# Order of the first stores and loads in an attention and mixture-of-experts kernel, and later batches in its last quad

## The reference

```
Q, K, V = xn @ W.T + bias           # 16 heads of 16 features
S[i, j] = K_i . Q_j / 4  + (-(i - j)), and -inf where j > i
s       = softmax(S) @ V, heads joined, @ o_w.T + o_b
probs   = softmax(xn @ gate_w); the best 2 of 8 experts, scores renormalised
f       = sum over the two experts of alpha_e * score * (gelu(xn @ fc1_e + b1_e) @ fc2_e + b2_e)
out     = x + s * silu(f)
```

## Time and profile before

| | |
|---|---|
| median of 3 runs | 718.47 us (714.88 to 721.5) |
| the profiled execution | 721.25 us |
| its span in the trace | 719.4 us |
| TensorE busy in the span | 681.2 us (95%) |
| VectorE, ScalarE, POOL busy | 535.6, 484.8, 236.3 us |
| bytes moved by DMA | 124.46 MB, 173 GB/s in the mean |

### The profile page before, as it was taken

How to read it: one execution, slowest core, us unless ns; L and a number is a source line. 1 busy time by engine, 2 the same in 40 slices (tenths; PEclk the granted TensorE clock), 3 DMA queues, 4 the chain that set the end, 5 groups by cost and what they waited for, 6 DMA issues and landing times.

```text
span 719.4 us, 17538 instructions
## 1 busy us (share of the span) xinstructions
PE 681.2 (95%) x6042; PEld 460.7 (64%) x6042; DVE 535.6 (74%) x1146; ACT 484.8 (67%) x994; POOL 236.3 (33%) x336
## 2 busy tenths in 40 slices
PE   6994999999999999999999999999789999999985
PEld 4873766555565556556555655654359998999764
DVE  6563887999989999998998999896224554444298
ACT  4551443677877877788787778878776666666374
POOL 5331211234023424323342432300034757566300
PEclk9996999999999999999999999999999999999998
DMA  6899976243765686477568657610369786955396
GB/s 213 267 259 312 330 225 200 79 65 87 106 138 138 136 173 148 124 170 156 137 140 174 140 130 164 166 28 19 89 132 259 255 195 219 233 182 174 121 391 248
DMA packets 74903, 124.46 MB, mean 173 GB/s; under 512 B 14184, under 2 KB 44392, under 8 KB 74696
## 3 DMA queue, kind: packets, MB, share of 16 engines
q1 hardware_dynamic: 65200, 95.17, 51.9%
q0 software_dynamic: 9616, 28.17, 12.7%
HBM read 72.56 MB, written 49.72 MB: 170 GB/s over the span
## 4 chain that ended last, share of the span: by engine, by line
PE 81%; DVE 9%; DMA 4%; issue 3%; ACT 2%; POOL 0%; SPq 0%; POOLq 0%; DVEq 0%; ACTq 0%
PE ps L1588 20%; PE ps L1519 14%; PE ps L1572 13%; PE ps L1676 8%; PE ps L1698 8%; PE ps L1508 7%; PE ps L1468 5%; DVE mxa L1111 3%; PE ps L1478 3%; PE ps L1659 2%; DVE x_room L1425 1%; DVE arena L1420 1%; DMA q_parts<-arena 1%; DVE arena L1410 1%; DMA arena<-xs_dram 1%
## 5 line engine op out<-in xcount | busy, mean ns | idle before, releaser
L1111 DVE TENSOR_REDUCE mxa<-ps 128x1 f32<-128x512 f32 (+3 forms) x608 | 358.3, 655 | 45.4 <-PE ps L1508 30.9
L972 ACT ACTIVATE arena<-ps 128x512 f32<-128x512 f32 x576 | 303.7, 603 | 83.1 <-PE ps L1572 42.9
L1519 PE MATMUL ps<-aug 57*128 57x512 f32 (+3 forms) x768 | 218.6, 403 | 11.7 <-issue 9.1
L1572 PE MATMUL ps<-aug 59*128 59x512 f32 (+3 forms) x768 | 215.3, 398 | 0.5 <-ACT arena L972 0.5
L1588 PE MATMUL ps<-arena,v_q 128*32 128x512 f32 (+3 forms) x1536 | 154.4, 497 | 6.7 <-ACT arena L972 6.3
L1572 PEld LDWEIGHTS ps<-aug 59*128 59x128 f32 x768 | 109.4, 185 | 75.9 <-ACT arena L972 70.3
L1519 PEld LDWEIGHTS ps<-aug 57*128 57x128 f32 x768 | 110.0, 188 | 47.4 <-DVE mxa L1111 24.3
L867 POOL DMA_INDIRECT xs_dram<-arena,slot x64 | 62.6, 978 | 75.6 <-ACT arena L972 71.7
L894 POOL DMA_INDIRECT y_dram<-arena,y_row_of x71 | 69.4, 977 | 52.4 <-DVE y_row_of L1349 45.2
L1508 PE MATMUL ps<-key_mask,key_rows 64*128 64x64 bf16 (+2 forms) x704 | 79.7, 209 | 0.0
L1676 PE MATMUL ps<-arena 128*128 128x128 f32 x568 | 75.2, 275 | 0.0
(11 more groups left out here) (149 smaller groups left out, 642.1 us busy)
## 6 DMA issues: line engine op xcount, KB each, us to landing
aug<-k_parts SPq DMA_DIRECT2D x96, 128.0 KB
aug<-q_parts SPq DMA_DIRECT2D x96, 128.0 KB
arena<-xs_dram SPq DMA_DIRECT2D x71, 128.5 KB, 2.6
k_parts<-arena SPq DMA_DIRECT2D x16, 512.0 KB, 4.7
q_parts<-arena SPq DMA_DIRECT2D x16, 512.0 KB, 5.6
arena<-y_dram SPq DMA_DIRECT2D x16, 512.0 KB, 6.7
xn_dram<-arena SPq DMA_DIRECT2D x8, 512.0 KB, 6.3
a_dram<-arena SPq DMA_DIRECT2D x128, 32.0 KB
```

The source lines that it names most:

```text
L972: nc.scalar.activation(prob_slot(q, i), score_bank(q, i), ACT.Exp).then_inc(exp_done, 1)
L1111: nc.vector.tensor_reduce(dst, src, AX.X, ALU.max).then_inc(piece_used, 1)
L1519: ins = nc.tensor.matmul(banks[:, at_ * width:(at_ + 1) * width], k_aug[n][rows, hp, ib * P:(ib + 1) * P], q_aug[n][rows, hp, lo:lo + widt ...
L1572: ins = nc.tensor.matmul(out_[:, col0:col0 + hi - lo], q_aug[n][rows, h // SIDES_OF_ARRAY, jb * P:(jb + 1) * P], k_aug[n][rows, h // SIDES ...
```

## The change

It has five parts. `SIDES` becomes K m0, Q m0, K m1, Q m1. The stores of sequence 0's m0 parts count on semaphores of their own (`first_parts_out`), and all twelve loads of quad 0 are issued in one go at the end of chunk 1, when the two m0 stores of each half have landed. The late constants move from behind chunk 0 to behind chunk 5; the masks stay and get a semaphore of their own. The waits follow these moves: `parts_stored(b)` replaces `16 * 4 * (b + 1)`, the first item waits for `masks_in`, and the wait for `consts_in` stands before the windows on TensorE and VectorE. Six batches and a seventh of the last window are sent one to three units later.

```diff
-LAST_BATCH_AFTER = (6, 11, 15, 19, 23, 27, 31, NU - 1)
+LAST_BATCH_AFTER = (7, 13, 18, 22, 26, 30, 33, NU - 1)
...
+def parts_stored(b):
+
+    return 16 * (4 * (b + 1) - 2 * (b > 0))
...
-        SIDES = [(side, m) for side in range(2) for m in range(KT)]
+        SIDES = [(side, m) for m in range(KT) for side in range(2)]
...
-                                 parts[c][n]).then_inc(parts_out[c], 16)
-                    if b == PLAIN and c == 0 and n < 2:
-                        if n == 0:
-                            for half in range(CHUNKS):
-                                sp.wait_ge(parts_out[half], 16 * 4 * (PLAIN + 1))
-                        for g in range(NLOAD // 2 * n, NLOAD // 2 * (n + 1)):
-                            load_rows(0, 0, g)
-                    if n == (1 if b == PLAIN and c == 0 else 0) and more > 0:
+                                 parts[c][n]).then_inc(first_parts_out[c] if b == 0 and m == 0 else parts_out[c], 16)
+                    if n == 0 and more > 0:
                         store_normalised(i + 1, b + c, 1 - c)
                     if b in (PLAIN + 1, PLAIN + 2) and c == 0:
+                        if b == PLAIN + 2 and n == 0:
+                            for half in range(CHUNKS):
+                                sp.wait_ge(parts_out[half], parts_stored(1))
                         for g in range(NLOAD // 4 * n, NLOAD // 4 * (n + 1)):
                             load_rows(b - PLAIN, b - PLAIN, g)
+                if b == 0 and c == 1:
+                    for half in range(CHUNKS):
+                        sp.wait_ge(first_parts_out[half], 16 * 2)
+                    for g in range(NLOAD):
+                        load_rows(0, 0, g)
...
                     if b == 0 and c == 0:
+                        load_masks()
+                    if b == PLAIN + 1 and c == 1:
                         for name in LATE_CONSTS:
                             sp.dma_start(*loads[name]).then_inc(consts_in, 16)
-                        load_masks()
...
-                act.wait_ge(parts_out[c], 64 * b + 64)
+                act.wait_ge(parts_out[c], parts_stored(b))
+                if b == 1:
+                    act.wait_ge(first_parts_out[c], 16 * 2)
...
+                if i == 0 and m == 0 and side == 1:
+                    pe.wait_ge(weights_high, 3)
...
-                            pe.wait_ge(consts_in, 16 * NCONST)
+                            pe.wait_ge(masks_in, 16 * NMASK)
```

More of the change, by code:

```diff
@@ L179 @@
 LATE_CONSTS = ("num", "before", "alpha", "wo", "ob", "vb")
-NCONST = SIDES_OF_ARRAY * len(CONSTS) + len(LATE_CONSTS)
+NMASK = SIDES_OF_ARRAY * len(CONSTS)
+NCONST = len(LATE_CONSTS)
 DEEP = 4
@@ L418, in rows_of @@
             return slice(ROW_TILE * side, ROW_TILE * side + count)
-        ident_in = sem("ident_in"); key_in = sem("key_in"); x_second = sem("x_second"); x_half = [sem(f"x_half{n}") for n in range(2)]; xn_half = sem("xn_half"); weights_in = sem("weights_in"); consts_in = sem("consts_in")
+        ident_in = sem("ident_in"); key_in = sem("key_in"); x_second = sem("x_second"); x_half = [sem(f"x_half{n}") for n in range(2)]; xn_half = sem("xn_half"); weights_in = sem("weights_in"); masks_in = sem("masks_in"); consts_in = sem("consts_in")
         bias_ready = sem("bias_ready")
@@ L427, in attention_moe_kernel @@
         proj_done = sem("proj_done"); first_done = sem("first_done"); proj_out = sem("proj_out"); masks_clear = sem("masks_clear"); masks_set = sem("masks_set"); decays_in = [sem(f"decays_in{n}") for n in range(AUG)]
-        parts_out = [sem(f"parts_out{c}") for c in range(CHUNKS)]
+        parts_out = [sem(f"parts_out{c}") for c in range(CHUNKS)]; first_parts_out = [sem(f"first_parts_out{c}") for c in range(CHUNKS)]
         v_done = sem("v_done"); v_out = sem("v_out")
@@ L496, in load_masks @@
                     rows = slice(ROW_TILE * side + 1, ROW_TILE * (side + 1))
[L497 to L500, removed]
+                    sp.dma_start(key_mask[rows, :], mask_neg[0:HALF_P - 1, 0:HALF_P]).then_inc(masks_in, 16)
+                    sp.dma_start(query_mask[rows, :], mask_negT[1:HALF_P, 0:HALF_P]).then_inc(masks_in, 16)
+                    sp.dma_start(key_rows[rows, HALF_P:P], ident_b[0:HALF_P - 1, 0:HALF_P]).then_inc(masks_in, 16)
+                    sp.dma_start(query_rows[rows, HALF_P:P], ident_b[1:HALF_P, 0:HALF_P]).then_inc(masks_in, 16)
             weights = lambda w: w.rearrange("(k p) n -> p k n", p=P)
@@ L609, in _ @@
                     if b == 0 and c == 0:
+                        load_masks()
+                    if b == PLAIN + 1 and c == 1:
                         for name in LATE_CONSTS:
                             sp.dma_start(*loads[name]).then_inc(consts_in, 16)
-                        load_masks()
             for c in range(CHUNKS):
-                sp.wait_ge(parts_out[c], 16 * 4 * (B + 1))
+                sp.wait_ge(parts_out[c], parts_stored(B))
             def window(q, n):
@@ L955, in _ @@
                     chunk(b, c, (B - b) * CHUNKS - c - 1)
-            act.wait_ge(parts_out[0], 16 * 4 * (B + 1))
+            act.wait_ge(parts_out[0], parts_stored(B))
             def evacuate(q, c):
@@ L966, in window @@
                     if first and i == RING // 2:
-                        act.wait_ge(parts_out[1], 16 * 4 * (B + 1))
+                        act.wait_ge(parts_out[1], parts_stored(B))
                     before_ = NU * q + i - RING
@@ L1184, in after_step @@
                         s, item = next(ahead_of_windows)
-                        if s == 0:
-                            dve.wait_ge(consts_in, 16 * NCONST)
                         follow_item(0, 0, s, item)
@@ L1310, in follow @@
                     follow_item(q, first_item(q), i, item)
+            dve.wait_ge(consts_in, 16 * NCONST)
             follow(0, choose_experts(), ROUTE_FROM)
@@ L1651, in _ @@
             pe.wait_ge(ones_set, AUG)
+            pe.wait_ge(consts_in, 16 * NCONST)
             for q in range(NQ):
```

## The result

The changed kernel takes 712.6 us, the median of 17 executions (709.0 to 717.13, one of 1506.85 aside), against 718.11 of the kernel before in the same comparison (714.27 to 725.28). The ratio is 0.9925, 95% interval 0.9899 to 0.9950. That is 5.5 us faster, inside 1%, where 16 were forecast. Medians in this text are over all executions; the ratios leave out those more than 1.5% above the same kernel's fastest. The two profiled executions are further apart: 710.94 us, span 709.1, against 721.25 and 719.4 of before. So there are two questions: where the 5.5 us (or, profile against profile, 10.3) come from, and where the rest of the 16 went.

A forecast was written before the change was run, and what follows sets the result against it. TensorE was taken as the bound, busy 95% of the span. Part 1's 11 us plus Part 2's 5 make 16 off the profiled 721.25, so 705.25; against the median of 718.47, 702.5 us, range 697.5 to 709.5 (8 in 10).

The forecast's parts named there:

- Part 2: Last window: later batches keep ScalarE's exponentials running without gaps; taken as 5 us, bounds 3 to 5.4.
- The fifth tile: Expert stage: SP's load of this token tile could reach TensorE late by 0 to 1.5 us.
- Part 1: Prologue, chunk 4: earlier row loads remove TensorE's hole; 12.5 less 1.5 us, worth 11 us.
- rival 5: Chunk 4: TensorE was not waiting for the loads, so only Part 2 stays; 713.5 us, chance 0.04.
- the prediction's signs: Expected in the trace: loads at about 34, ScalarE's chunk 4 at 55 to 59, chunk 4 14 to 17 us, clock 1.00.
- The hole's price, 12.5 us: Chunk 4: TensorE's 9.06 us wait plus slow work at a lowered clock, all to be won.
- What is late next, 1.5 us charged: Chunk 4: ScalarE's wait for chunk 2's stores stalls TensorE 0 to 1 us; with VectorE's lag, 1.5 charged.
- the ledger: DMA queue from 33.6 on: 6.1 MB at 245 GB/s, chunk 2's last store landing at 55 to 58.4.
- rival 2: Chunk 4: the stall moves, ScalarE starting at 61 to 63; 704.5 to 709 us, chance 0.18.
- Rival 4: Chunk 4: the whole queue runs at 140 GB/s, deciding from 147 down; slower, 724 us, chance 0.03.
- No gain, as POOL is not what TensorE waits for: Prologue: chunk 2's xn store goes out at 40 instead of 51.9, freeing POOL earlier, for no gain.
- The prediction's 218 GB/s for a pair of loads: Row loads: estimated rate for pairs 64 partitions apart, 7.2 us for twelve; 109 GB/s for one load.

The follow-up runs named there:

- last_quad_only: The kernel before with only the new list of batches in its last window; 728.82 us, ratio 0.9925.
- xn_first: wait_per_part with chunk 3's store of xn issued ahead of the row loads; 707.12 us, ratio 0.9822 to the kernel before.
- xn_first_decays_later: xn_first with the second quad's constant rows loaded one chunk later; 705.78 us, ratio 0.9811 to the kernel before.
- xn_first_early_consts: xn_first with the late constants back after the first chunk; 724.92 us, ratio 0.9871 to the kernel before; run again, 708.33 us, 0.9881.
- decays_later_early_consts: xn_first_decays_later with the late constants back after the first chunk; 724.36 us, ratio 0.9869 to the kernel before.
- consts_only: The kernel before with only its late constants moved behind chunk 5; 718.49 us, ratio 0.9992.
- before_again: The kernel before, unchanged, profiled a second time; that execution took 714.85 us.
- wait_per_part: The changed kernel with one semaphore per store of parts, so ACT waits for each buffer's store alone; 727.05 us, ratio 0.9902 to the kernel before.
- xn_first_one_sum: The changed kernel with chunk 3's xn store ahead of the row loads, ACT still waiting for all four stores; 730.74 us, ratio 0.9946 to before.
- prologue_only: The changed kernel with the old list of batches in its last window; 733.61 us, ratio 0.9995 to the kernel before.
- loads_over_ports: The changed kernel with the twelve row loads reordered so three groups of 16 partitions take turns; 727.99 us, ratio 0.9943 to the kernel before.
- xn_first_again: xn_first, unchanged, run again in another group; 707.66 us, ratio 0.9859 to the kernel before.
- groups 1 and 3: Two of four sets of follow-up runs, each beside the kernel before on the same chip; there the kernel before took 734.14 and 734.23 us.
- after_again: The changed kernel, unchanged, run again; 728.43 us, ratio 0.9932 to the kernel before.
- groups 1 and 4: Two of four sets of follow-up runs, each beside the kernel before on the same chip; there the kernel before took 734.14 and 718.7 us.

## Why the prediction was right and wrong

**Part 2 held, in the changed kernel's profile to the tenth.** 5.4 us of ScalarE's idle time go, the exponentials run in one piece, the expert stage begins 5.4 us earlier than the window's start alone would give. The fifth tile was not late (L1672 at 525.88, no wait) and POOL caught up: from 521.49 to the end of the span are 187.6 us, and 187.5 before. By itself it gives 5.3 us in medians, last_quad_only. Not every execution keeps all of it. From SP's last load of the maxima to the expert stage proper are 31.9 us in the four profiles with the old list and 26.5 or 26.6 in nine with the new one, but 28.0 to 29.6 in the other four with it (xn_first, xn_first_decays_later, xn_first_early_consts, decays_later_early_consts). From there to the end are 187.5 to 188.5 us with the old list and 187.3 to 190.6 with the new; last_quad_only has 189.9. That the change costs this was not shown.

**Part 1's mechanism held, its two terms did not.** The loads went out at 34.97 (34 forecast), the hole went, chunk 5 did not change, and nothing waits for constants or masks. That TensorE had waited for the loads, which the row did not name and rival 5 doubted, the packets show: the twelve loads are the trace's 384 packets of 4096 bytes, and the last of them ends at 54.77 to 61.54 in the four profiles with a hole, 1.0 to 1.8 us ahead of the first item (61.54 and 62.97 in the first profile); in the changed kernel it ends at 48.50, inside the 46 to 49 of the forecast, and the item goes at 53.57. Of the prediction's signs, ACT's first part of chunk 4 came at 60.30 (55 to 59 forecast), chunk 4 lasted 19.99 us (14 to 17), and the clock did not stay at 1.00. Two steps failed:

*The hole's price, 12.5 us.* It was right for the one execution that was profiled, and I took it for the kernel. The three other profiles with the old place of the loads and early constants have holes of 2.82, 4.00 and 4.43 us, and consts_only has none. In the first profile the loads' packets also took longer, 16.3 us against 11.9 to 13.6 in these three. By before_again the term is 21.78 - 15.3 = 6.5 us. And I took the same 16 us off the median, though the profiled execution lay 2.8 us above it, without asking where that execution was slow: it was slow in the very place that the change mends. The times shown already gave a hint: the lowest, 714.88, lies 6.4 us below the profiled one. before_again took 714.85, and it is ahead by just these 6.4 us after window 0 (141.38 against 147.81).

*What is late next, 1.5 us charged.* The stall was put at 0 to 1 us, with chunk 2's last store landing at 55 to 58.4. It landed at 60.28. The rate was better than taken: 284 GB/s from 33.6 to 60.28, not 245. But that is 7.6 MB, not 6.1. By the bytes of the trace's packets some 0.7 MB of the difference belong to two stores of chunk 1 issued before 33.6 (landed at 34.91 and 36.15), which the ledger took for done, and some 0.8 MB to chunk 3's stores, issued from 45.43 on: they share the engines with chunk 2's, and I had let the queue serve in order. TensorE lost 2.8 us idle and 1.9 to the clock in chunk 4 (19.99 - 15.31 = 4.7 in all). This is rival 2, which had 0.18: it gave ACT's start as 61 to 63, a loss of 3.5 to 5.5 (up to 8 with the clock), and 704.5 to 709 from the same oversized hole, so its time was missed too. Rival 4's sum does not close either: its own terms break even at about 160 GB/s and not at 147, and its 724 lies within the 7.2 us that the prediction counts as no change.

*"No gain, as POOL is not what TensorE waits for."* Wrong in the end. POOL's wait for the xn store was hidden behind ACT's, and wait_per_part and xn_first_one_sum show the two side by side: lift one, and the other holds TensorE. Lifting only the xn wait gave nothing (0.9946 beside 0.9932), only ACT's at most some of it (0.9902), both 0.9822, 0.9859 when it ran again, and 0.9869 to 0.9881 with early constants.

*Given back later.* Window 0 took 1.1 us more after the change (35.02 against 33.93) and the windows 1 to 14 another 1.65. Neither is a cost of the change that the runs could pin down: window 0 took 33.5 to 33.9 us in the two profiles of the kernel before, and 33.97 and 37.56 in two of xn_first.

With both terms corrected, 6.5 - 4.7 = 1.8 us for the prologue and 5.4 for the window make 7.2 us; less the 1.5 us that window 0 took more than in before_again (35.02 against 33.51), 5.7, where 5.5 were measured. That it comes so near is partly luck, as each term is from one profile or two. Still open is how often the hole of before is long. The medians of before lie 3.3 us above before_again's execution, so it is not always short; but prologue_only, which has no hole, gained only 0.5 us against a group's median. One profile of each can't say what the other executions lost.

**The rule on ports** was weighed in the prediction. The Trainium skill (SBUF — State Buffer, Door 1: The DMA port swizzle) ties DMA bandwidth to the number of ports that the partitions reach. The prediction's 218 GB/s for a pair of loads was a step of its own: the same page of the Trainium skill, under Can I just issue two DMAs to hit both halves?, says that two concurrent DMAs, at partitions 0 and 64, gained only 6% over a single one. Here another order brought nothing (loads_over_ports: ACT's wait 8.44 us against 7.56 and 8.17, and the loads' packets took 12.7 us against 12.4 and 12.2 in the two profiles of the changed kernel). But neighbours went to different groups in either order, and loads and stores ran together, with a DMA share of 1.05 from 35 to 46 us at 218 GB/s. So no run here tests the rule.

## What to carry to other kernels

A wait that is removed ahead of busy DMA engines is only worth what the transfers behind it allow: list each buffer whose store stands behind the loads that are moved up, who refills it, and lift all those waits together. Here the change of the prologue gave nothing that shows without that; with it, and the constants left early, its loads and order of stores gave 4 to 8 us. Try the parts of a change alone: the constants' move by itself already took the hole away in its profile. Before pricing a stall from one profile, set that execution against the other times of the kernel: if it is slow among them, the stall may be what made it slow, and the difference belongs to that term.

## What the runs showed of the hardware that was not expected

While the DMA engines' share is above 1.0, issuing one store of 512 KB took SP up to 6.25 us in the changed kernel, and 8.77 in xn_first, where 0.4 is usual. Another store of the changed kernel took 17.05 us from issue to landing, where the median was 5.3 and the longest 14.6 in the kernel before. SP's queue in xn_first:

```profile
50.77 8.77 SPq L538 DMA_DIRECT2D k_parts<-arena  x1
```

A halving of the clock costs by where it falls. Window 0 has a stretch at 0.50 in all seventeen profiles. In xn_first it lasts from 127 to about 140, VectorE is left without work (0.04 us in the first row), and the window takes 37.56 us; in xn_first_again, the same kernel, it lies from about 117 to 124 and the window takes 33.97. Rows of stretches of xn_first, then of xn_first_again:

```profile
132.00:134.00 2.00, 2.00 (x15) 0.94 (x7) 0.04 (x1) 0.11 (x1) 1.87 (x5) 0.50 0.00 0
...
136.00:138.00 2.00, 2.00 (x14) 0.70 (x11) 1.97 (x5) 1.09 (x2) 0.00 (x0) 0.50 0.00 0
```

```profile
122.00:124.00 2.00, 2.00 (x16) 0.92 (x17) 2.00 (x6) 1.49 (x3) 0.00 (x0) 0.50 0.03 8
124.00:126.00 2.00, 1.93 (x30) 1.13 (x22) 1.62 (x6) 0.99 (x3) 0.00 (x0) 0.97 0.00 0
```

The longer last windows of four profiles, named above, are of the same kind. In xn_first TensorE was busy 1.57 us of 2 from 490 to 492 and all of the time from 492 on, and the clock still fell to 0.50 from 496 to 498; the exponentials wait 2.08 us there, against 0.80 in xn_first_again, whose clock is 1.00 throughout.

In groups 1 and 3 windows 4 to 12 take some 26.3 us instead of 25.0, at a granted clock of 1.00, and window 13 takes 27.7 to 29.4. The rows are of after_again, in group 3, and of the changed kernel's first profile. Windows 0 to 2 and window 14 are as long in both. The cause is open; the record gives groups 1 and 4 the same chip number, 8, though only group 1 is slow. The change's ratio was the same in either, 0.9925 and 0.9932.

```profile
244.00:270.00 26.00, 25.69 (x277) 14.74 (x275) 22.75 (x42) 19.78 (x38) 8.46 (x13) 1.00 0.60 145
```

```profile
242.00:267.00 25.00, 24.88 (x283) 14.33 (x280) 22.92 (x43) 19.77 (x38) 8.81 (x13) 1.00 0.65 150
```
